# ScalarE's counts of a mask moved apart from its checks of rows, in a four-layer graph kernel

## The chip, the cores and the metric
One core of a Trainium2 chip runs the kernel. The metric is the device time of one execution in microseconds; the times shown are medians of several executions.

## The reference
Four graph layers on x (8 batches, 2048 nodes, 64 channels) share one row-normalised adjacency matrix `adj` (2048 x 2048). Each layer is followed by x = layernorm(x + layer(x)). Cut to what matters:
```
L0: w = einsum(emb, weight); x_g = [x, A x, 2 A (A x) - x]; out = x_g w + b
L1: att = softmax(where(adj > 0.5, leaky_relu(s1 + s2), -9e15)); out = elu(att h)
L2: emb = x W^T + b;  out = ((A + I) emb) / rowsum(A + I)
L3: v = x, row 0 of v set to a given value; 3 times:
        h = relu([v, A v] W1^T + b1);  v = h W2^T + b2
```

## The kernel before, in words
All nonzero values of a row of `adj` are equal in the expected inputs, so the kernel keeps a mask `Bm` in 8-bit floats (0 or 64) with one factor per row, and multiplies by the mask. Since it must be right for other matrices too, it checks this on the way. For each of the 16 blocks of 128 rows (`it` = 0 to 15) ScalarE makes three passes over 2048 columns, each with a sum per row:

- `chk`: counts the mask's entries of block `it` (a Copy of `Bm[:, it, :]` into `junk`, sum in `cnt`);
- then, in the step `sgn`, a Relu of the row block minus the row's maximum (sum in `over`, output into `junk`), and
- a Sign of the same difference (sum in `sg1`, output over the row buffer itself).

The row blocks of `adj` come by a DMA into one buffer, `rowt`. SyncE issues the load of block it + 1 when the Sign of block `it` is done (`s_sign`). `junk` and `rowt` lie in the memory of layer 0's weights and are free when layer 0's last product is done (`s_zp`). After all checks VectorE sums up (`flags`), TensorE adds over partitions (`total`), VectorE decides (`verdict`), and all engines branch: to a slow general program, or to the rest of the fast one.

The order of the work is written out by hand as one list of steps, `MIDDLE` and then `TAIL`. Each engine walks through the whole list in order and issues its own part of every step; semaphores tie the parts together. `last_order` makes `TAIL`. It counts in half-steps of about 4 us: 0 to 31 are layer 2, with the 16 products of the mask, `P` k = 0 to 15 (two half-steps for each, four pieces for each product), and 32 to 115 are layer 3, with the pieces `M` of seven-product sums. `at(y, ...)` puts a step at half-step y, `on(h, ...)` at half-step 32 + h. Steps put at one half-step keep the order in which they were put, the ones left over from `MIDDLE` first.

The steps named below:

- `E` k: takes product k out of PSUM. ScalarE writes the high half into `T`, then VectorE the low half (semaphore `s_zl`). Products have three PSUM banks, and P k waits for E k-3.
- `W` (c, j): TensorE multiplies what E 4c+j made by a weight (it waits for `s_zl`), and VectorE adds it to X.
- `sq`, `red`, `var`, `root`, `rs`, `apply` (L, c, j): the norm of layer L. ScalarE squares, VectorE sums, ScalarE takes the root, VectorE makes the factor and applies it.
- `row_a`, `row_b`, `addrow`: the row that layer 1 adds (an Exp on ScalarE).
- `split` (c, j): when the apply of layer 1 is done, ScalarE writes the high half of X for layer 2's products; GpSimd writes the low half and adds a bias.
- `rows`: nine small steps of VectorE that prepare factors.
- `v0` (c, j): the same halves for layer 3's first input. ScalarE, then GpSimd; TensorE's `D` (c, j) waits for GpSimd's part.
- `G`, `mix`, `cut`, `V`, `t22`: layer 3's passes. G multiplies by a weight and VectorE takes the result out; mix forms the sums; ScalarE and GpSimd cut them into halves; V and t22 take products out of PSUM.

ScalarE's part of chk and sgn before (the whole stands in the listing):
```
elif kind == "chk":
    e.wait_ge(s_zp, 8 * NT)
    if it: e.wait_ge(s_over, it)
    fn(junk, Bm[:, it, :], ACT.Copy, accum_out=cnt[...]).then_inc(s_cnt, 1)
elif kind == "sgn":
    e.wait_ge(s_land, 16 * (it + 1)); ...; e.wait_ge(s_cnt, it + 1)
    fn(junk, rowt, ACT.Relu, ...).then_inc(s_over, 1)
    e.wait_ge(s_over, it + 1)
    fn(rowt, rowt, ACT.Sign, ...).then_inc(s_sign, 1)
```

Of the kernel before, what the change touches and what calls it, by code (L numbers as in the profile page):

```python
# [177 lines left out]
def last_order(after):  # L178
# [42 lines left out]
        at(y + 5, *mixes(n, 1, 4), cut(n, 1, "S1"))  # L221
        at(y + 6, cut(n, 1, "S3"), cut(n, 1, "S4"))
    for it in range(NT):
        at(12 + 4 * it if it < 5 else 32 + 4 * (it - 5) - (it - 5) // 4, ("chk", it))
        at(14 + 4 * it if it < 5 else 34 + 4 * (it - 5) - (it - 5) // 4, ("sgn", it))
    for k in range(16):
        p = pieces("P", k)
        order += late.pop(2 * k, []) + (p[0:2] if k else []) + late.pop(2 * k + 1, []) + (p[2:4] + [("E", k)] if k else [])
    for n in (4, 5, 6, 7):
# [13 lines left out]
        on(h + 14, cut(n, 1, "S1"))  # L243
        on(h + 15, cut(n, 1, "S3"))
        on(h + 16, cut(n, 1, "S4"))
    on(44, ("flags",))
    on(46, ("total",))
    on(47, ("verdict",))

    for n, s, jj, h in ((6, 1, 0, 61), (6, 1, 1, 62), (6, 4, 0, 69), (6, 4, 1, 70), (6, 5, 0, 71), (6, 5, 1, 72), (6, 6, 0, 72),  # L250
                        (6, 6, 1, 73), (7, 1, 0, 75), (7, 1, 1, 76), (7, 4, 0, 80), (7, 4, 1, 81)):
# [50 lines left out]
def gnn_kernel(nc, x_in, at_in, a_in, embt_in, sm_in, bx_in, w0_in, a12_in, w0bb_in, out):  # L302
    ctx = ExitStack()
    with ctx:
# [376 lines left out]
                    RSN[norm_key(x)] = len(RSN)  # L681

        number_norms()

        ORDER3 = [ending(n, s, jj) for n in (6, 7) for s in ENDS for jj in range(2)]

# [379 lines left out]
        def scalar_steps(e, steps):  # L1066
# [3 lines left out]
            for step in steps:  # L1070
# [15 lines left out]
                elif kind == "Z":  # L1086
                    u, t = step[1:]
                    c, j = divmod(u, 4)
                    n4, it = 4 * u + t, 4 * j + t
                    if n4:  # L1090
                        e.wait_ge(s_ab, n4)
                    for g in range(2):
                        e.wait_ge(s_acc[0], 5 * n4 + (3, 5)[g])
                        e.wait_ge(s_acc[1], 5 * n4 + (2, 5)[g])
                        ps = zpair(2 * n4 + g)
                        for d in range(DV, 8):
                            fn(grid(AT[:, 3 * g + d - DV, :]), ps[:, :, d, :], ACT.Copy,
                               scale=emb[:, it, 8 * g + d:8 * g + d + 1]).then_inc(s_za, 1)
                elif kind == "sq":
                    L, c, j = step[1:]  # L1100
                    u = 4 * c + j
                    if L == 0:
                        e.wait_ge(s_add, 4 * u + 4)
                    else:
                        e.wait_ge((None, s_y1, s_y2, s_y3)[L], (order3(c, j) if L == 3 else u) + 1)
                    if L == 3 and summed_by_act(c, j):
                        r = order3(c, j) // 2
                        if r >= 2:
                            e.wait_ge(s_rs, RSN[first_of(*ORDER3[2 * r - 4])] + 1)
                            e.wait_ge(s_sq, SQN[L, c, j])  # L1110
                        o, q = four(sq_buf(L, c, j)), st_part(L, c, j, 0)
                        for i in range(8):
                            t, d = i // 2, slice(64 * (i % 2), 64 * (i % 2) + 64)
                            m = fn(o[:, t, d], X[:, 4 * j + t, 128 * c + d.start:128 * c + d.stop], ACT.Square, accum_out=q[:, i:i + 1])
                        m.then_inc(s_sq, 1)
                        continue
                    if L == 3:
                        e.wait_ge(s_sq, SQN[L, c, j])
                        if order3(c, j) == 15:
                            e.wait_ge(s_red, REDN[(3, *ORDER3[13])] + 1)  # L1120
                    elif SQPREV[L, c, j] is not None:
                        e.wait_ge(s_red, REDN[SQPREV[L, c, j]] + 1)
                    fn(four(sq_buf(L, c, j)), xpart(c, j), ACT.Square).then_inc(s_sq, 1)
                elif kind in ("root", "root3") or kind == "var" and step[1] < 2:
                    L, c, j = (*norm_key(step), 0)[:3]
                    m = 2 if L == 3 else 1
                    e.wait_ge(s_var, VARN[norm_key(step)] + 1)
                    fn(st_part(L, c, j, 1, m), st_part(L, c, j, 2, m), ACT.Sqrt).then_inc(s_sd, 1)
                elif kind == "row_a":
                    e.wait_ge(s_neg, step[1] + 1)  # L1130
                    fn(ROW[:, 1, :], ROW[:, 1, :], ACT.Exp).then_inc(s_exp, 1)
                elif kind == "split":
                    c, j = step[1:]
                    e.wait_ge(s_p2, 4 * c + 4)
                    e.wait_ge(s_n[1], 4 * c + j + 1)
                    fn(spart(0, c, j), xpart(c, j), ACT.Copy).then_inc(s_sh, 1)
                elif kind == "E":
                    k = step[1]
                    c, j = divmod(k, 4)
                    e.wait_ge(s_p, k + 1)  # L1140
                    fn(T[:, c, 0, block(j)], bank(product_bank(k)), ACT.Copy, scale=1.0 / EDGE).then_inc(s_zh, 1)
                elif kind == "V" and step[2] in (0, 2, 6):
                    n, s, jj = step[1:]
                    p = n // 2
                    e.wait_ge(s_p, slot_done(n, s, jj))
                    if RTW[step] is not None:
                        e.wait_ge(s_gl, RTW[step])
                    if n == 2 and s < 6:

                        e.wait_ge(s_red, REDN[2, 1 + s, 3] + 1)  # L1150
                    o, i = RT[rt_buf(s, jj)], bank(pair_bank(n, s, jj))
                    if s == 6:
                        fn(o, i, ACT.Relu, scale=col(cKG + p)).then_inc(s_gt, 1)
                    else:
                        fn(o, i, ACT.Copy, scale=col(cKG + p)).then_inc(s_cp, 1)
                elif kind == "t22":
                    n, jj = step[1:]
                    e.wait_ge(s_t2, 2 * (n - 2) + jj + 1)
                    if RTW[step] is not None:
                        e.wait_ge(s_gl, RTW[step])  # L1160
                    fn(RT[rt_buf(3, jj)], bank(aux_bank[step]), ACT.Copy, scale=col(cKG + n // 2)).then_inc(s_cp, 1)
                elif kind == "cut":
                    n, jj, what = step[1:]
                    if what[0] == "X":
                        e.wait_ge(s_ut, GN[(n // 2, *block_of(n, jj, what))] + 1)
                    else:
                        e.wait_ge(s_mx, MN["mix", n, jj, what] + 1)

                    if what in ("S1", "S2", "S3"):
                        if n > 2:  # L1170
                            e.wait_ge(s_p, slot_done(n - 1, {"S2": 2, "S1": 3, "S3": 4}[what], 1))
                    elif n >= 4:
                        e.wait_ge(s_p, slot_done(n - 2, [x[0] for x in SLOTS].index(what), 1))
                    else:
                        c, j = block_of(n, jj, "X21" if what == "S4" else what)
                        e.wait_ge(s_d, 4 * c + j + 1)
                    fn(half_of(n, what, 0, jj), four(made(n, jj, what)), ACT.Copy).then_inc(s_uh, 1)
                elif kind == "v0":
                    c, j = step[1:]
                    e.wait_ge(s_p, 4 * c + 4)  # L1180
                    e.wait_ge(s_n[2], 4 * c + j + 1)
                    if j == 0:
                        e.wait_ge(s_vt, c + 1)
                        fn(stile(0, 0, c), V0T, ACT.Copy)
                        fn(S[:, 0, 1:4, chunk(c)], X[:, 1:4, chunk(c)], ACT.Copy).then_inc(s_vh, 1)
                    else:
                        fn(spart(0, c, j), xpart(c, j), ACT.Copy).then_inc(s_vh, 1)
                elif kind == "D":
                    c, j = step[1:]
                    e.wait_ge(s_d, 4 * c + j + 1)  # L1190
                    fn(T[:, c, 0, block(j)], bank(aux_bank[step]), ACT.Copy, scale=1.0 / EDGE).then_inc(s_dh, 1)
                elif kind == "chk":
                    it = step[1]
                    e.wait_ge(s_zp, 8 * NT)
                    if it:
                        e.wait_ge(s_over, it)
                    fn(junk, Bm[:, it, :], ACT.Copy, accum_out=cnt[:, it:it + 1]).then_inc(s_cnt, 1)
                elif kind == "sgn":

                    it = step[1]  # L1200
                    e.wait_ge(s_land, 16 * (it + 1))
                    e.wait_ge(s_nr, 1)
                    e.wait_ge(s_cnt, it + 1)
                    fn(junk, rowt, ACT.Relu, bias=nr[:, it:it + 1], accum_out=over[:, it:it + 1]).then_inc(s_over, 1)
                    e.wait_ge(s_over, it + 1)
                    fn(rowt, rowt, ACT.Sign, bias=nr[:, it:it + 1], accum_out=sg1[:, it:it + 1]).then_inc(s_sign, 1)

# [1054 lines left out]
```

## Time and profile before
| what | value |
|---|---|
| median of 3 executions | 1042.79 us (1041.26 to 1042.98) |
| the profiled execution | 1043.06 us, span of its instructions 1041.3 us |
| TensorE busy | 1012.3 us (97%) |
| VectorE busy | 678.1 us (65%) |
| GpSimd busy | 552.9 us (53%) |
| ScalarE busy | 456.8 us (44%) |
| mean granted clock of TensorE | 0.994 |

The busy time of an engine counts its instructions, not its waits. "Idle before", in brackets behind a row of a timeline, is the time in which the engine had nothing to do ahead of that instruction, with the instruction whose end released it. PE is TensorE, ACT is ScalarE, DVE is VectorE, POOL is GpSimd. L1068, L1219 and L1737 are lines of helpers that issue most instructions of ScalarE, VectorE and GpSimd, so a step is recognised by its tiles, its shape and its place in the order.

### The profile page before, as it was taken

The numbers are of one execution on the slowest core, as the hardware profiler recorded it, in microseconds if no ns is written. First come the engines' busy times: TensorE is split into PE (matmuls) and PEld (weight loads), VectorE is DVE, ScalarE is ACT, GpSimd is POOL, SyncE is SP. The second block draws the span as 40 slices with busy tenths as digits, with TensorE's granted clock in tenths as the row PEclk, the third lists the DMA queues.
The fourth block names the chain that finished last, engine by engine and source line by source line (L and its number), as shares of the span: only waits on it lengthen the run. The fifth ranks groups of instructions, "written<-read, shape, count | busy, mean of one in ns | idle before, by whom it ended". The sixth has DMA issues, their size and how long they took to land. (4 is left out here: it accounts for less than half of the span.)

```text
span 1041.3 us, 18648 instructions
## 1 busy us (share of the span) xinstructions
PE 1012.3 (97%) x6854; PEld 486.3 (47%) x6854; DVE 678.1 (65%) x1683; ACT 456.8 (44%) x1109; POOL 552.9 (53%) x645
## 2 busy tenths in 40 slices
PE   7999999999999999999999999999999999999995
PEld 3445444444444444434445556454554545455553
DVE  4877565657566786687667775776584545547556
ACT  4632323333334543444333575584766532232632
POOL 0005497766658798879878374464443242323311
PEclk9999999999999999999999999999999999999998
DMA  9930000000000000000010121121221100000022
GB/s 371 404 127 1 2 1 2 1 2 1 1 1 2 2 1 2 1 2 1 1 42 1 41 82 42 41 82 41 82 82 50 72 1 2 3 2 21 21 62 61
DMA packets 14658, 45.65 MB, mean 44 GB/s; under 512 B 960, under 2 KB 9280, under 8 KB 10080
## 3 DMA queue, kind: packets, MB, share of 16 engines
q1 hardware_dynamic: 14560, 44.39, 11.5%
q8 instruction: 56, 0.92, 0.4%
q14 instruction: 42, 0.34, 0.1%
HBM read 40.19 MB, written 4.19 MB: 43 GB/s over the span
## 5 line engine op out<-in xcount | busy, mean ns | idle before, releaser
L788 PE MATMUL PS<-BW,S 128*128 128x512 fp8e4 x1280 | 291.9, 380 | 0.7 <-DVE R L1219 0.7
L1068 ACT ACTIVATE T<-PS,SM 128x128 f32<-128x128 f32 x384 | 112.8, 365 | 234.3 <-DVE X L1219 155.9
L918 PE MATMUL PS<-WZ,R 64*128 64x512 f16 x1536 | 198.0, 377 | 1.2 <-ACT T L1068 1.2
L788 PEld LDWEIGHTS PS<-BW,S 128*128 128x128 f16 x1280 | 120.6, 98 | 150.3 <-issue 18.2
L955 PE MATMUL PS<-BW,S 128*128 128x512 fp8e4 x768 | 173.1, 379 | 0.6 <-POOL T L1737 0.6
L1737 POOL TENSOR_TENSOR T<-T 128x128 f32<-128x128 f32 (+1 forms) x192 | 124.3, 647 | 74.4 <-ACT T L1068 64.3
L1219 DVE SCALAR_TENSOR_TENSOR X<-PS,SM,X 128x128 f32<-128x128 f32 x320 | 109.5, 342 | 76.4 <-PE PS L918 76.4
L918 PEld LDWEIGHTS PS<-WZ,R 64*128 64x128 f16 x1536 | 69.5, 94 | 104.1 <-issue 26.3
L955 PEld LDWEIGHTS PS<-BW,S 128*128 128x128 f16 x768 | 73.7, 98 | 83.9 <-issue 1.1
L955 PE MATMUL PS<-BW,T 128*128 128x512 fp8e4 x480 | 109.5, 379 | 1.3 <-POOL T L1737 1.3
L1737 POOL TENSOR_TENSOR S<-R,S 128x512 f16<-128x512 f32 (+1 forms) x46 | 52.3, 1144 | 105.6 <-ACT S L1068 105.5
L1219 DVE SCALAR_TENSOR_TENSOR T<-PS,SM,T 128x128 f32<-128x128 f32 x256 | 87.7, 343 | 27.1 <-PE PS L918 27.1
L918 PE MATMUL PS<-WZ,T 64*128 64x512 f16 x768 | 103.8, 376 | 0.0
L1737 POOL TENSOR_TENSOR T<-R,T 128x512 f16<-128x512 f32 x40 | 49.3, 1240 | 87.6 <-DVE T L1211 44.8
L1219 DVE SCALAR_TENSOR_TENSOR R<-PS,cs,R 128x512 f32<-128x512 f32 x48 | 36.0, 749 | 64.1 <-PE PS L955 32.7
L1761 POOL TENSOR_TENSOR BW<-BW 128x512 fp8e4<-128x512 fp8e4 x64 | 70.9, 1113 | 2.7
L955 PEld LDWEIGHTS PS<-BW,T 128*128 128x128 f16 x480 | 46.2, 98 | 54.4 <-POOL T L1737 1.8
L1219 DVE SCALAR_TENSOR_TENSOR R<-PS,ra,R 128x128 f32<-128x128 f32 x176 | 48.8, 342 | 33.6 <-PE PS L775 21.8
L1068 ACT ACTIVATE R<-PS,cs 128x512 f32<-128x512 f32 x48 | 32.6, 679 | 83.7 <-PE PS L782 52.5
L1068 ACT ACTIVATE WZ<-WZ,ra 128x2048 f16<-128x2048 f32 (+1 forms) x32 | 63.9, 1996 | 1.3 <-DMA WZ<-a_in 0.8
L1737 POOL TENSOR_TENSOR X<-X,T 128x128 f32<-128x128 f32 x128 | 58.4, 457 | 10.0
L773 PE MATMUL PS<-hat,T 128*128 128x128 f16 x320 | 57.8, 221 | 4.2 <-DVE T L1219 2.5
(210 smaller groups left out, 1518.9 us busy)
## 6 DMA issues: line engine op xcount, KB each, us to landing
WZ<-a_in SPq DMA_DIRECT2D x16, 1024.0 KB, 4.8
BW<-at_in SPq DMA_DIRECT2D x8, 1024.0 KB, 18.4
R<-at_in SPq DMA_DIRECT2D x7, 1024.0 KB, 12.7
out<-X SPq DMA_DIRECT2D x16, 256.0 KB, 2.3
X<-x_in SPq DMA_DIRECT2D x3, 1024.0 KB, 19.6
T<-w_in SPq DMA_DIRECT2D x1, 1536.0 KB, 15.4
R<-at_in SPq DMA_DIRECT2D x2, 512.0 KB, 4.7
SM<-sm_in SPq DMA_DIRECT2D x1, 520.5 KB, 17.9
```

The lines of the kernel that those rows point to most:

```text
L773: e.matmul(ok, th, hat[:, 0, kind, :], start=True, stop=False)
L788: m = e.matmul(o, stile(h, t, c), Bm[:, t, block(j)], start=(t == 0 and h == 0), stop=(last and t == NT - 1 and h == 1))
L918: m = e.matmul(bank(b0 + q), halves[kd][zh][r, :], WZ[r, wh, kd, block(g)], start=(i == 0), stop=(i == 8))
L955: m = e.matmul(o, half_of(n, what, h, q % 2)[:, t, :], b[:, 4 * (q % 2) + t, :], start=(s in (0, 1, 3) and q % 2 == 0 and t == 0 and h == ...
L1068: return e.activation(o, i, f, **kw)
L1219: return e.scalar_tensor_tensor(out=o, in0=a, scalar=s, in1=b, op0=f, op1=g)
L1737: return e.tensor_tensor(o, a, b, f)
L1761: e.tensor_tensor(o, a, b, f, saturate=False).then_inc(s_bt, 1)
```

## The change: counts early, checks of rows in two steps
The step sgn becomes two, `ovr` (the Relu) and `sgn` (the Sign), and chk, ovr and sgn get other places in the list. In half-steps: chk of block it was at 12, 16, 20, 24, 28, 32, 36, ... and is now at 2 + it, so 2 to 17. ovr and sgn together were two half-steps behind chk (14, 18, ... up to 72); now ovr is at 10, 13, 16, 19 for blocks 0 to 3 and at 51, 53, 56, 58, 61, 64, 66, 69, 71, 74, 77, 79 for the others, and sgn one half-step behind each. `flags`, `total` and `verdict` move from 44, 46 and 47 of layer 3 to 49, 51 and 52; the branch stays at 56. Since chk and ovr both write junk, a function now finds for each of them the one ahead of it in the list, whose semaphore it waits for.
```diff
     for it in range(NT):
-        at(12 + 4 * it if it < 5 else 32 + 4 * (it - 5) - (it - 5) // 4, ("chk", it))
-        at(14 + 4 * it if it < 5 else 34 + 4 * (it - 5) - (it - 5) // 4, ("sgn", it))
+        at(2 + it, ("chk", it))
+        y = 10 + 3 * it if it < 4 else 51 + (13 * (it - 4)) // 5
+        at(y, ("ovr", it))
+        at(y + 1, ("sgn", it))
...
-    on(44, ("flags",))
-    on(46, ("total",))
-    on(47, ("verdict",))
+    on(49, ("flags",))
+    on(51, ("total",))
+    on(52, ("verdict",))
...
+        JUNK = {}
+        def number_junk():
+            held = None
+            for x in TAIL:
+                if x[0] in ("chk", "ovr"):
+                    JUNK[x] = held
+                    held = (s_cnt if x[0] == "chk" else s_over, x[1] + 1)
+        number_junk()
...
                 elif kind == "chk":
                     it = step[1]
                     e.wait_ge(s_zp, 8 * NT)
-                    if it:
-                        e.wait_ge(s_over, it)
+                    if JUNK[step] is not None:
+                        e.wait_ge(*JUNK[step])
                     fn(junk, Bm[:, it, :], ACT.Copy, accum_out=cnt[:, it:it + 1]).then_inc(s_cnt, 1)
-                elif kind == "sgn":
+                elif kind == "ovr":
                     it = step[1]
                     e.wait_ge(s_land, 16 * (it + 1))
                     e.wait_ge(s_nr, 1)
-                    e.wait_ge(s_cnt, it + 1)
+                    e.wait_ge(*JUNK[step])
                     fn(junk, rowt, ACT.Relu, bias=nr[:, it:it + 1], accum_out=over[:, it:it + 1]).then_inc(s_over, 1)
+                elif kind == "sgn":
+                    it = step[1]
                     e.wait_ge(s_over, it + 1)
                     fn(rowt, rowt, ACT.Sign, bias=nr[:, it:it + 1], accum_out=sg1[:, it:it + 1]).then_inc(s_sign, 1)
```

## Rows read from the trace of the kernel before
**Rows 1.** Page, part 1: busy us, share of the span, instructions
```profile
PE 1012.3 (97%) x6854; PEld 486.3 (47%) x6854; DVE 678.1 (65%) x1683; ACT 456.8 (44%) x1109; POOL 552.9 (53%) x645
```
**Rows 2.** TensorE's timeline: start, us, what, [idle before <-released by]
```profile
600.76 0.22 PE L763 MATMUL PS<-dg,S 128*128 128x128 f16 x1 [3.14 <-POOL S L1737]
...
668.49 0.23 PE L773 MATMUL PS<-hat,T 128*128 128x128 f16 x1 [1.69 <-DVE R L1219]
...
686.74 0.39 PE L780 MATMUL PS<-T,hat 128*128 128x512 f16 x1 [0.52 <-DVE T L1219]
...
706.09 0.23 PE L763 MATMUL PS<-dg,S 128*128 128x128 f16 x1 [1.39 <-DVE SM L1219]
...
747.26 1.04 PE L955 MATMUL PS<-BW,T 128*128 128x512 fp8e4 x4 [1.27 <-POOL T L1737]
```
**Rows 3.** Windows: length; PE, PEld, DVE, ACT, POOL busy; granted clock; DMA
```profile
538.64:597.35 58.71, 58.71 (x394) 31.60 (x393) 43.97 (x91) 25.85 (x41) 38.01 (x34) 1.00 0.06 19
...
601.40:604.80 3.40, 3.40 (x18) 1.81 (x16) 1.17 (x2) 2.20 (x4) 1.48 (x2) 0.50 0.24 67
668.50:671.90 3.40, 3.40 (x25) 1.94 (x26) 3.38 (x4) 0.08 (x1) 1.55 (x2) 1.00 0.00 0
```
**Rows 4.** ScalarE's groups by shape, 525 to 860 us: busy, mean ns, idle before
```profile
L1068 ACT ACTIVATE WZ<-BW 128x2048 f16<-128x2048 fp8e4 x16 | 30.4, 1899 | 0.0
...
L1068 ACT ACT_TABLE_LOAD x3 | 3.8, 1283 | 0.1
```
**Rows 5.** ScalarE's timeline, 538 to 597 us (T<-PS is an E, S<-X a split)
```profile
538.64 0.58 ACT L1068 ACTIVATE T<-PS 128x512 f16<-128x512 f32 x1
543.19 0.63 ACT L1068 ACTIVATE S<-X 128x512 f16<-128x512 f32 x1 [3.97 <-DVE X L1531]
...
547.49 0.60 ACT L1068 ACTIVATE T<-PS 128x512 f16<-128x512 f32 x1 [1.14 <-PE PS L938]
...
555.51 0.60 ACT L1068 ACTIVATE T<-PS 128x512 f16<-128x512 f32 x1 [4.86 <-PE PS L938]
559.90 0.63 ACT L1068 ACTIVATE S<-X 128x512 f16<-128x512 f32 x1 [3.79 <-DVE X L1531]
...
564.45 0.60 ACT L1068 ACTIVATE T<-PS 128x512 f16<-128x512 f32 x1 [1.78 <-PE PS L938]
...
569.39 1.90 ACT L1068 ACTIVATE WZ<-BW 128x2048 f16<-128x2048 fp8e4 x1
...
571.28 0.61 ACT L1068 ACTIVATE R<-X 128x512 f32<-128x512 f32 x1
...
573.49 0.58 ACT L1068 ACTIVATE T<-PS 128x512 f16<-128x512 f32 x1
...
577.40 1.99 ACT L1068 ACTIVATE WZ<-WZ,ra 128x2048 f16<-128x2048 f32 x1
...
581.51 0.57 ACT L1068 ACTIVATE T<-PS 128x512 f16<-128x512 f32 x1
...
590.86 0.31 ACT L1068 ACTIVATE S<-R 128x128 f16<-128x128 f32 x1 [2.91 <-DVE R L1219]
...
596.30 1.67 ACT L1068 ACTIVATE S<-X 128x512 f16<-128x512 f32 x3 [4.23 <-DVE X L1531]
```
**Rows 6.** VectorE's timeline: E 4, and the squares' sum after the long idle time
```profile
558.52 0.69 DVE L1219 SCALAR_TENSOR_TENSOR T<-PS,T 128x512 f16<-128x512 f32 x1
...
659.60 0.69 DVE L1222 TENSOR_REDUCE T<-R 128x8 f32<-128x512 f32 x1 [5.24 <-ACT R L1068]
```
**Rows 7.** GpSimd's timeline: low half of split(3,1), then v0(0,1) and v0(0,2)
```profile
597.00 1.16 POOL L1737 TENSOR_TENSOR S<-X,S 128x512 f16<-128x512 f32 x1 [2.55 <-ACT S L1068]
...
599.46 2.27 POOL L1737 TENSOR_TENSOR S<-X,S 128x512 f16<-128x512 f32 x2
```
**Rows 8.** DMA issues: KB each, median us from issue to landing
```profile
WZ<-a_in SPq DMA_DIRECT2D x16, 1024.0 KB, 4.8
```

## The prediction, made before the changed kernel ran
> **What bounds the kernel now.** I read the page's busy times first: TensorE is busy for 97% of the span and ScalarE for 44% [rows 1]. So TensorE's work sets the time, the change takes none of it away, and only what TensorE waits for can change. I next looked through TensorE's timeline for idle time behind the point where layer 2 begins (about 525 us). The reader is to see five waits there [rows 2]: 3.14 us at 600.76, and 1.69, 0.52, 1.39 and 1.27 us at 668.49, 686.74, 706.09 and 747.26. The first one costs more than its length: from 601.40 to 604.80 the granted clock is 0.50, the 1.2 GHz level, and 3.4 us of work at half speed are 1.7 us of loss; after the wait of 1.69 us it stays at 1.00, the 2.4 GHz level [rows 3]. Then I read ScalarE's own timeline where layer 2 begins [rows 5], because it is the only engine whose order changes, and beside it the steps of VectorE and GpSimd that hand work back and forth with it [rows 6, 7].
>
> **What the change moves.** No operation is added or dropped. ScalarE still runs 16 counts (chk) and 16 pairs (ovr, sgn). A count takes 1.90 us [rows 4] and holds the queue for 1.9 us (569.39 to 571.28); a pair holds it for 4.1 us (577.40 to 581.51), so about 2.1 and 2.0 us for its halves [rows 5]. What changes is which steps stand behind them. All 16 counts go to half-steps 2 to 17, two before nearly every E k, the step that takes product k out of PSUM. Pairs 0 to 3 go to half-steps 10 to 20, none follows up to 50, and the other 12 go to 51 to 80.
>
> **What goes away.** Between half-steps 21 and 50 ScalarE has no checks, and the four later waits lie there. Take the one at 668.49: VectorE had stood idle for 5.24 us until 659.60, for a square that ScalarE had behind pair 4; it caught up too late for the PSUM bank that TensorE wanted [rows 2, 6]. Without that pair (4.1 us) VectorE comes some 2.8 us earlier there, more than the 1.69 us. The waits at 706.09 and 747.26 follow pairs 6 and 8 in the same way, and the short one pair 5. I take all four away: 1.69 + 0.52 + 1.39 + 1.27 = 4.87 us.
>
> **What the 16 counts cost.** ScalarE has 58.71 - 25.85 = 32.9 us of idle time between E 1 and the row v0(0,1) [rows 3], and looks able to hide them. But VectorE takes its steps in order too. In a loop that runs through the window, ScalarE's E k lets VectorE do its E k and then an apply, which lets ScalarE do its next split; behind that split the new order puts two counts, and E k+1 behind them. A count ahead of an E therefore delays the loop itself, and the wait for VectorE's apply comes afterwards just as before. I carried the delay along the queue, starting from the times in [rows 5]:
> - E 1 (538.64) has two counts ahead: +3.8 us. VectorE's E 1, its rs and apply move by as much, so split(2,0) goes from 543.19 to 547.0.
> - E 2 has two more: +7.6. E 3 has two more, but had been waiting for TensorE, so 547.49 becomes 557.6: +10.1.
> - E 4 (555.51) has two more, less its old idle time: +8.9. VectorE comes to it only behind the step rows, which moved by 10.1, so it goes on at 568.6 in place of 558.52 [rows 6], and split(2,3) at 570.0 in place of 559.90.
> - E 5 (564.45) has ovr 0, count 8, sgn 0 and count 9 ahead, 7.9 us: it comes at 580.6, +16.1.
> - E 6 (573.49) has count 10, ovr 1 and count 11 ahead: 590.8, +17.4.
> - E 7 (581.51) has sgn 1 and counts 12 and 13 ahead, and lost the old pair 0: 600.5, +19.0.
> - v0(0,0) (590.86) has ovr 2 and count 14 ahead, in place of one count: +19.0. E 8 has sgn 2 and count 15: 614.4.
> - VectorE then makes the row for split(3,1), which goes from 596.30 to 616.4: +20.1.
>
> GpSimd follows as in [rows 7]: low half and bias of split(3,1) from 597.00, low half of v0(0,1) from 599.46 (half of 2.27 us, so to 600.6), which is what released TensorE at 600.76. All of it moves by 20.1 us. TensorE can run ahead only in part: W(1,0) needs E 4 and stands right behind product 5 (whose end is E 5's old start, 564.45), W(1,1) needs E 5 behind product 6, and so on. So the time will not be lost in one place. I expect waits of about 4.3 us before W(1,0), 4.6 before W(1,1), 2.3 before W(1,2), 1.7 before W(1,3), and about 10.6 in D(0,0) and D(0,1); the last includes the old 3.14. The sum over the old waits is 20.1 us.
> Two adjacent operations on the junk buffer also wait for each other. Where ovr and Sign do so now, 2.1 us lie between them and only 2.0 behind, so I add 0.1 us at each of 8 such places: 0.8 us.
>
> **What could come behind it.** After 21 us of delay TensorE is behind ScalarE's remaining work by more than before (E 9 moves by about 18 us), and only pair 3 is left there, so I book no new wait up to half-step 50. The clock: several waits are now over 3.14 us, but what is lost after the earlier ones is waited out anyway; the last costs 1.7 us as it does today. Zero net, and at most another 1.7 us if it stays low twice as long. In half-steps 51 to 80 pairs come every 2.6 half-steps, and five times ovr stands one half-step behind the Sign that frees the row buffer. A row needs 4.8 us to land [rows 8], so ScalarE waits 3 to 4 us there and cuts come up to 9 us later. The PSUM evictions among them move by 3 us or less, and the cuts are wanted 15 us or more later; the kernel of before has no wait of TensorE there at all between 750 and 900 us though each pair holds 4.1 us in one piece. I take nothing, and 4 us as the upper end. flags, total and verdict move five half-steps, some 20 us; the verdict is at 52 and the branch at 56, so four half-steps of cover (some 16 us) are left: nothing.
>
> On the activation tables, first the trace: a load takes 1.28 us, with three in this stretch [rows 4], and after the last one all Sign and Sqrt steps run on it. Sign 0 now stands between the row step's Exp and the Sqrt of var(1,3), so that last load may only come earlier, ahead of sgn 0, where the queue is full; that would be 1.3 us more. The Trainium skill, page "ScalarE: Activation LUTs", section "What ACT_TABLE_LOAD costs", puts a switch of sets at 2.66 us with its drain, by which it would be 2.7 us. The trace has 1.28. I leave it out of the sum and in the range.
>
> **Sum.** 20.1 + 0.8 - 4.9 = +16.0 us. The profiled execution took 1043.06 us around its span of 1041.3, so it becomes 1059.1; it was 0.27 us above the median of 1042.79, so I predict 1059.
>
> **Rivals.**
> *Hidden counts, so the kernel gets faster.* If VectorE and GpSimd absorb the delays, that is if the 32.9 us of idle time really take the counts, only ScalarE's full queue counts: 25.85 - 7.9 (checks that are there now) + 16 x 1.95 + 3 x 4.2 = 61.8 us against 58.71, and v0(0,1) comes 3.1 us later. Then 3.1 - 4.9 = -1.8: 1041. It decides below a delay of 4.9 us. For it speaks ScalarE's idle time; against it that each idle stretch in [rows 5] sits behind a step which waits for VectorE, and that VectorE's step waits for the E behind the counts. If the old wait of 3.14 went too, with its clock loss, 1033. Chance 0.10.
> *No measurable change.* A delay of 3 to 7 us, eaten by the 4.9: 1041 to 1045. Chance 0.05.
> *Half absorbed.* Work that TensorE's waits give room for shortens VectorE's steps, and the delay is 8 to 13 us: 1046 to 1051. Chance 0.13.
> *Forecast.* In-order queues pass it all on: 1052 to 1063. Chance 0.64.
> *The late pairs cost too.* The waits for rows in half-steps 51 to 80 reach TensorE, or the table load does: 16.0 + 4 + 1.3 = 21: 1064. Chance 0.08.
>
> **The numbers.** A difference under 0.2% (2 us) can't be told from none here. Faster 0.11, same 0.04, slower 0.85. The range goes from 1046, below which are the first two rivals, to 1064.
>
> **What would show it.** In the profile after: TensorE's waits before the W products between 565 and 600, and a long one until GpSimd's low half of v0(0,1) near 620; ScalarE nearly without idle time from 565 to 615; no waits where the four were. If the first wait is still near 601 and about 3 us long, the loop argument is wrong, and the kernel is level or faster.

## The result, and the profile after

The changed kernel takes 1054.06 us (median of 4 executions, 1053.1 to 1055.02), beside 1042.52 us for the kernel before on the same chip: a ratio of 1.0114, with an interval of 1.0099 to 1.013. It is slower by 11.5 us, where +16.0 was forecast. The profiled execution took 1055.02 us, around a span of 1053.2.

The page's busy times of the kernel after, as in [rows 1]:
```profile
PE 1014.5 (96%) x6854; PEld 487.7 (46%) x6854; DVE 673.6 (64%) x1683; ACT 457.0 (43%) x1109; POOL 553.4 (53%) x645
```
The instruction counts are the same as before. The span is 11.9 us more than 1041.3. TensorE is idle for 1053.2 - 1014.5 = 38.7 us, before for 29.0: +9.7. Its busy time rose by 2.2, and 9.7 + 2.2 = 11.9.

TensorE's timeline of the kernel after, all its waits behind the start of layer 2; they answer to [rows 2]:
```profile
565.85 0.22 PE L788 MATMUL PS<-hat,T 128*128 128x128 f16 x1 [1.13 <-issue]
...
578.48 0.22 PE L788 MATMUL PS<-hat,T 128*128 128x128 f16 x1 [4.44 <-issue]
...
588.70 0.22 PE L788 MATMUL PS<-hat,T 128*128 128x128 f16 x1 [0.36 <-issue]
...
598.59 0.22 PE L788 MATMUL PS<-hat,T 128*128 128x128 f16 x1 [1.70 <-issue]
...
608.78 0.22 PE L778 MATMUL PS<-dg,S 128*128 128x128 f16 x1 [2.02 <-POOL S L1755]
...
617.50 0.26 PE L778 MATMUL PS<-dg,S 128*128 128x128 f16 x1 [8.11 <-POOL S L1755]
```
The first four rows are the W products (their input is T), the last two D(0,0) and D(0,1). Together they wait 17.76 us where 3.14 stood, +14.6. Behind 617.50 there is none up to 900: the four waits of 4.87 us in all are gone. 14.6 - 4.9 = +9.7, the idle time above. The word "issue" must not be taken to mean that nothing was waited for. VectorE's timeline in the same stretch:
```profile
565.06 0.69 DVE L1237 SCALAR_TENSOR_TENSOR T<-PS,T 128x512 f16<-128x512 f32 x1
...
577.68 0.69 DVE L1237 SCALAR_TENSOR_TENSOR T<-PS,T 128x512 f16<-128x512 f32 x1 [3.79 <-ACT T L1083]
```
These are VectorE's parts of E 4 and E 5. They end at 565.75 and 578.37, and the W products start 0.10 and 0.11 us later: the W steps waited for `s_zl`. The second row also names what VectorE had waited for: ScalarE's part of E 5.

ScalarE's timeline, kernel after; it answers to [rows 5]:
```profile
538.28 1.90 ACT L1083 ACTIVATE WZ<-BW 128x2048 f16<-128x2048 fp8e4 x1
...
540.36 1.91 ACT L1083 ACTIVATE WZ<-BW 128x2048 f16<-128x2048 fp8e4 x1
...
542.26 0.58 ACT L1083 ACTIVATE T<-PS 128x512 f16<-128x512 f32 x1
545.54 0.63 ACT L1083 ACTIVATE S<-X 128x512 f16<-128x512 f32 x1 [2.70 <-DVE X L1549]
...
566.44 0.63 ACT L1083 ACTIVATE S<-X 128x512 f16<-128x512 f32 x1 [2.25 <-DVE X L1549]
567.09 1.28 ACT L1083 ACT_TABLE_LOAD   x1
568.38 0.31 ACT L1083 ACTIVATE ROW<-ROW 128x128 f32<-128x128 f32 x1
...
573.20 1.99 ACT L1083 ACTIVATE WZ<-WZ,ra 128x2048 f32<-128x2048 f32 x1
...
577.08 0.57 ACT L1083 ACTIVATE T<-PS 128x512 f16<-128x512 f32 x1
...
587.89 1.28 ACT L1083 ACT_TABLE_LOAD   x1
...
613.03 1.67 ACT L1083 ACTIVATE S<-X 128x512 f16<-128x512 f32 x3 [1.42 <-DVE X L1549]
```
Two counts (BW into WZ, which here is Bm into junk) stand ahead of E 1 at 542.26, and ahead of split(2,0) at 545.54 ScalarE still waits 2.70 us for VectorE's apply: the counts did not fill that gap, they moved it. (It was 3.97 us before; the 1.27 us between are VectorE's step rs, which took that much less.) The last row is split(3,1), 16.7 us later than in [rows 5]. GpSimd's low halves behind it, which release D(0,1), answer to [rows 7]:
```profile
613.74 1.15 POOL L1755 TENSOR_TENSOR S<-X,S 128x512 f16<-128x512 f32 x1 [3.60 <-ACT S L1083]
...
616.19 3.39 POOL L1755 TENSOR_TENSOR S<-X,S 128x512 f16<-128x512 f32 x3
```

Windows around the last two waits and the second one, kernel after (stretch, length, busy us of PE, PEld, DVE, ACT, POOL with instruction counts, granted clock, DMA share, GB/s); they answer to [rows 3]:
```profile
538.28:613.57 75.29, 61.46 (x396) 32.35 (x394) 40.37 (x91) 59.97 (x76) 36.96 (x33) 0.95 0.12 43
...
609.70:617.50 7.80, 0.00 (x0) 0.03 (x1) 3.99 (x8) 6.38 (x9) 4.12 (x5) 0.50 0.37 134
617.50:623.30 5.80, 5.80 (x29) 3.41 (x30) 3.82 (x6) 3.79 (x8) 4.37 (x4) 0.50 0.00 0
578.90:582.40 3.50, 3.50 (x16) 1.58 (x14) 3.16 (x10) 2.72 (x4) 2.61 (x3) 0.51 0.14 59
```
The clock is at 0.50, the 1.2 GHz level, for 3.4 us behind the wait of 4.44, and from 609.7 to 623.4, the last 5.9 us of it with work. ScalarE is busy for 59.97 of 75.29 us from its first count to split(3,1): over the whole stretch it was not full. From 565 to 615, where the prediction wanted it nearly without idle time, it is busy for 41.38 of 50 us.

The stretch behind D(0,1), first the kernel before, then the kernel after, with the same 2714 matmuls:
```profile
600.76:1041.30 440.54, 423.91 (x2714) 222.82 (x2714) 272.76 (x614) 217.31 (x490) 169.74 (x143) 0.98 0.13 44
...
617.50:1053.20 435.70, 424.45 (x2714) 223.93 (x2714) 271.66 (x614) 182.80 (x455) 170.96 (x143) 0.98 0.12 40
```
D(0,1) starts 16.7 us later, and from there to the end the kernel is 4.8 us shorter: 16.7 - 4.8 = 11.9, the growth of the span.

### The profile page after: what moved, and what is told of

It is laid out like the page before. It is cut to its first block, busy times and chain, and to the rows that moved or that the text cites. A ratio compares the mean times of both kernels' runs of the same rounds, so it can differ in the third digit from the quotient of the medians.

```text
span 1053.2 us, 18648 instructions
## 1 busy us (share of the span) xinstructions
PE 1014.5 (96%) x6854; PEld 487.7 (46%) x6854; DVE 673.6 (64%) x1683; ACT 457.0 (43%) x1109; POOL 553.4 (53%) x645
## 4 chain that ended last, share of the span: by engine, by line
PE 80%; DVE 9%; ACT 6%; issue 2%; DMA 2%; POOL 1%; SPq 0%; ACTq 0%; DVEq 0%; POOLq 0%
PE PS L970 27%; PE PS L933 23%; PE PS L803 20%; ACT WZ L1083 3%; DMA BW<-at_in 2%; PE PS L788 2%; PE PS L790 2%; PE PS L789 2%; DVE BW L1234 1%; DVE T L1237 1%; DVE X L1549 1%; PE PS L797 1%; PE PS L795 1%; PE PS L796 1%; DVE X L1237 1%
## 5 line engine op out<-in xcount | busy, mean ns | idle before, releaser
L1083 ACT ACTIVATE WZ<-WZ,ra 128x2048 f16<-128x2048 f32 (+1 forms) x32 | 63.8, 1993 | 27.5 <-DMA WZ<-a_in 27.5
L788 PE MATMUL PS<-hat,T 128*128 128x128 f16 x320 | 58.2, 221 | 10.1 <-issue 7.6
L1237 DVE SCALAR_TENSOR_TENSOR T<-PS,T 128x512 f16<-128x512 f32 x48 | 32.0, 686 | 53.0 <-ACT T L1083 48.0
## 6 DMA issues: line engine op xcount, KB each, us to landing
SM<-sm_in SPq DMA_DIRECT2D x1, 520.5 KB, 17.8
```

The lines of the kernel that those rows point to most:

```text
L788: e.matmul(ok, th, hat[:, 0, kind, :], start=True, stop=False)
L1083: return e.activation(o, i, f, **kw)
L1237: return e.scalar_tensor_tensor(out=o, in0=a, scalar=s, in1=b, op0=f, op1=g)
```

## The experiments

Each kernel was compared with the kernel before on the same chip. The kernel before read 1042.1 to 1042.5 us in all of these comparisons, so differences of a few tenths between two rows of the table mean nothing. "Shift" is how much later split(3,1) starts than the 596.30 of [rows 5], in us; the last column is TensorE's last wait before 625, in us.

| kernel | median us | ratio, interval | shift | last wait |
|---|---|---|---|---|
| after | 1054.06 | 1.0114, 1.0099 to 1.013 | +16.7 | 8.11 |
| e1 counts behind E | 1046.8 | 1.0042, 1.0025 to 1.0059 | +9.9 | 8.27 |
| e2 no counts | 1036.72 | 0.9937, 0.9919 to 0.9954 | +0.26 | 3.02 |
| e3 pairs only | 1036.41 | 0.994, 0.9924 to 0.9957 | +0.25 | 3.02 |
| e4 counts only | 1053.81 | 1.0108, 1.0091 to 1.0125 | +12.6 | 7.06 |
| e5 one behind E | 1039.7 | 0.9976, 0.9967 to 0.9986 | +2.2 | 5.32 |
| e6 one ahead of E | 1044.61 | 1.0026, 1.0016 to 1.0037 | +8.0 | 8.11 |
| e7 mask sums later | 1039.46 | 0.9972, 0.9963 to 0.9982 | -1.6 | 1.15 |
| e8 pairs, D later | 1032.73 | 0.9909, 0.9896 to 0.9923 | -0.17 | 1.34 |
| e9 e8 and e7 | 1033.18 | 0.9917, 0.9903 to 0.9931 | -1.75 | 1.4 |

**e1, the two counts directly behind E k.** On the kernel after:
```diff
-        at(2 + it, ("chk", it))
...
+        if 1 <= k <= 8:
+            order += [("chk", 2 * k - 2), ("chk", 2 * k - 1)]
```


> The changed kernel, but each pair of counts stands directly behind its E k (k = 1 to 8) in place of ahead of it; the same 16 counts beside the same products, pairs as changed. Loop theory (what costs is that a count stands between ScalarE's split and the E that VectorE waits for): VectorE gets its E at once and makes the apply while ScalarE counts, so split(3,1) comes about 8 us earlier than in the changed kernel, the waits of TensorE before W products shrink to under 3 us in all, and the time is 1043 to 1048 us. Rival, ScalarE's load (its queue is simply full in that stretch, wherever the counts stand): as the changed kernel, 1052 to 1055 us.

The split comes 6.8 us less late than in the kernel after, and the kernel is 7.3 us faster, with the same load on ScalarE beside the same products. So load alone doesn't explain the loss. But order alone doesn't either: the split is still 9.9 us late. ScalarE's timeline of e1 at split(2,0) and split(2,1) shows no wait for VectorE any more where 3.97 and 1.42 us stood, since two counts fill more than that:
```profile
542.79 0.63 ACT L1084 ACTIVATE S<-X 128x512 f16<-128x512 f32 x1
...
547.79 0.61 ACT L1084 ACTIVATE S<-X 128x512 f16<-128x512 f32 x1
```
The waits at the W products shrink to 1.1 us in all. The long wait at D(0,1) stays, in TensorE's timeline of e1:
```profile
610.64 0.26 PE L779 MATMUL PS<-dg,S 128*128 128x128 f16 x1 [8.27 <-POOL S L1756]
```

**e2, no counts at all.** This kernel leaves out the 16 counts; `flags` then takes a difference of `sg1` with itself, so the check of the mask's entries isn't made.
```diff
-        at(2 + it, ("chk", it))
...
-                    e.wait_ge(s_cnt, NT)
-                    fc(stt(e, cw2, cnt, 1.0 / EDGE, sg1, ALU.mult, ALU.subtract))
+                    fc(stt(e, cw2, sg1, 1.0, sg1, ALU.mult, ALU.subtract))
```


> The changed kernel without the 16 counts of the mask (that part of the check is left out, and the sum over it is made from zero). Loop theory: pairs 0 to 3 at half-steps 10 to 20 cost TensorE nothing new (the old wait of about 3 us near 600 stays), and the four later waits stay away: 1036 to 1039 us, so the counts' price is 15 to 18 us. Rival, the pairs at half-steps 10 to 20 are a good part of the loss: 1042 us or more.

TensorE's only wait from 560 to 900 is the old one:
```profile
601.03 0.22 PE L777 MATMUL PS<-dg,S 128*128 128x128 f16 x1 [3.02 <-POOL S L1754]
```
Against the kernel after, the 16 counts cost 1054.06 - 1036.72 = 17.3 us, and what is left of the change, the moved pairs, gains 5.5.

**e3, the pairs only.** The counts back at their old places, pairs and flags as changed.
```diff
-        at(2 + it, ("chk", it))
+        at(12 + 4 * it if it < 5 else 32 + 4 * (it - 5) - (it - 5) // 4, ("chk", it))
...
```


> Only ovr and sgn (and flags, total, verdict) go to their new places; the counts stay at 12, 16, 20, ... as before. Loop theory: ahead of split(3,1) stand 12.4 us of halves of pairs and 3.8 us of counts in place of 7.9 us, partly taken by idle time: 4 to 6 us later; the four later waits (4.9 us) go: 1040 to 1044 us, no difference from before that can be told. Rival, half-steps 51 to 80 are too full with counts and halves of pairs waiting for rows to land: new waits of TensorE there, 1045 us or more.

I missed the size: 1036.41, faster than expected. I had put the split 4 to 6 us later. The halves of pairs 0 to 2 put E 5 and E 6 2.6 and 2.4 us later, but E 7 only 0.3 and v0(0,0) 0.25: idle time took it all up. The wait at D(0,1) is the old one, 3.02 us at 601.01 as in e2, and the later ones are gone. It takes as long as e2, which has no counts. So with the pairs moved, the 16 counts cost nothing at their old places and 17.3 us at their new ones.

**e4, the counts only.** Counts as changed; ovr, sgn, flags, total and verdict at their old places.
```diff
-        y = 10 + 3 * it if it < 4 else 51 + (13 * (it - 4)) // 5
-        at(y, ("ovr", it))
-        at(y + 1, ("sgn", it))
+        at(14 + 4 * it if it < 5 else 34 + 4 * (it - 5) - (it - 5) // 4, ("ovr", it), ("sgn", it))
...
```


> Only the counts go to half-steps 2 to 17; each pair, flags, total and verdict stay where they were. Loop theory: up to v0(0,1) the queue lacks ovr and sgn 1 and 2 (8 us) of the changed kernel, so TensorE passes D(0,1) 8 to 10 us later than before, not 16.7, and of the later waits most stay, as they come from pairs: 1048 to 1053 us. Rival, the later waits come from the sum of checks and go with the counts: 1046 us or less.

The shift was 12.6, more than the 8 to 10 that I had put down, and the time 0.8 us over the upper end. TensorE's timeline of e4 has the long wait, and the first of the four later ones again:
```profile
613.39 0.26 PE L776 MATMUL PS<-dg,S 128*128 128x128 f16 x1 [7.06 <-POOL S L1753]
...
681.36 0.23 PE L786 MATMUL PS<-hat,T 128*128 128x128 f16 x1 [1.70 <-DVE R L1235]
```
So the removal of those waits is the pairs' doing. From here to the kernel after, three pairs stand ahead of split(3,1) in place of one, some 8 us of work, of which 4.1 us arrive in the shift; and e4's later waits go (1.70, 0.51, 1.03 and 0.28, 3.5 us in all); the two times agree within 0.3 us.

**e5 and e6, one count behind or ahead of E k.** Both have the pairs as changed, one count at each of E 1 to E 15 and the 16th at the start of layer 3. They differ by the order of two neighbours on ScalarE alone.
In e5, behind the line that appends E k:
```diff
-        at(2 + it, ("chk", it))
...
+        if k:
+            order.append(("chk", k - 1))
...
+    on(0, ("chk", 15))
```
In e6 the list of the two steps `[("chk", k - 1), ("E", k)]` stands in the place of E k instead.


> The changed kernel with one count per product, directly behind E k (k = 1 to 15, the 16th at the start of layer 3), pairs as changed. Loop theory: 1.9 us of count fit into ScalarE's idle time behind nearly every E (3.97, 1.42, 1.42, 3.79 us before the splits), so split(3,1) comes 0 to 4 us later than before: 1036 to 1041 us. Rival, ScalarE's load from ovr and sgn 0 to 3 plus any counts there is what costs: half the counts beside the pairs, half the loss, 1045 us.

> The same as the run with one count per product behind E k, but each count directly ahead of E k. The load on ScalarE is the same, only the order of two neighbours differs. Loop theory: each count ahead of an E delays VectorE's E by 1.9 us wherever ScalarE has no idle time before it, so split(3,1) comes 6 to 10 us later than before, 4 us or more later than with the counts behind: 1041 to 1047 us. Rival, load: no difference between the two.

Both came out as expected. e6 loses 4.9 us to e5, from one swap. And e5, against e1, says what the number of counts is worth when all stand behind E: one for each product in place of two is 7.1 us faster (1039.7 against 1046.8). ScalarE's timeline, first e5:
```profile
538.66 0.58 ACT L1085 ACTIVATE T<-PS 128x512 f16<-128x512 f32 x1
539.14 1.90 ACT L1085 ACTIVATE WZ<-BW 128x2048 f16<-128x2048 fp8e4 x1
...
543.22 0.63 ACT L1085 ACTIVATE S<-X 128x512 f16<-128x512 f32 x1 [2.08 <-DVE X L1551]
543.75 0.58 ACT L1085 ACTIVATE T<-PS 128x512 f16<-128x512 f32 x1
```
and e6:
```profile
538.72 1.89 ACT L1083 ACTIVATE WZ<-BW 128x2048 f16<-128x2048 fp8e4 x1
...
540.61 0.58 ACT L1083 ACTIVATE T<-PS 128x512 f16<-128x512 f32 x1
543.88 0.63 ACT L1083 ACTIVATE S<-X 128x512 f16<-128x512 f32 x1 [2.70 <-DVE X L1549]
544.41 1.89 ACT L1083 ACTIVATE WZ<-BW 128x2048 f16<-128x2048 fp8e4 x1
...
546.31 0.57 ACT L1083 ACTIVATE T<-PS 128x512 f16<-128x512 f32 x1
```
Behind E 1 the count runs while VectorE works towards the apply, and E 2 starts at 543.75. Ahead of E 1 it runs while VectorE waits for E 1, the wait of 2.70 us for the apply comes on top, and E 2 starts at 546.31.

**e7, the sums of the mask later.** This one asks why the delay was smaller than forecast. It is the kernel before, with 16 of GpSimd's mask sums (`bt`) moved out of the stretch.
```diff
-        at(i - 46, ("bt", i))
+        at(i - 46 + 16, ("bt", i))
```


> The kernel before, with GpSimd's last 16 mask sums (bt 48 to 63, 1.1 us each) put 16 half-steps later; everything else as before. Theory: VectorE's small steps (rs, rows) are slow while GpSimd works beside them, so in this run the step rows takes 3.5 to 4.5 us in place of 6.2 and rs(1,2) 1.2 to 1.6 us in place of 2.5. Rival, they take as long for another reason (their own waits on each other): unchanged. The time: within 2 us of before, since E 4 and E 5 wait for TensorE anyway.

It is 2.7 us faster, where I had given it at most 2, and the step rows came out shorter than the 3.5 to 4.5 us that I expected. GpSimd has nothing to do from 553.09 to 558.68, while VectorE makes most of the step rows, and VectorE's timeline of e7 reads
```profile
554.07 0.31 DVE L1212 TENSOR_SCALAR R<-SM,cs 128x64 f32<-128x64 f32 x1
554.42 0.67 DVE L1212 TENSOR_SCALAR R<-c1row,cs 128x64 f32<-128x64 f32 x2
```
The same three instructions in the kernel before, VectorE's timeline:
```profile
555.11 1.27 DVE L1212 TENSOR_SCALAR R<-SM,cs 128x64 f32<-128x64 f32 x1
556.42 2.07 DVE L1212 TENSOR_SCALAR R<-c1row,cs 128x64 f32<-128x64 f32 x2
```
and GpSimd's beside them:
```profile
555.07 1.26 POOL L1737 TENSOR_TENSOR X<-X,bc 128x512 f32<-128x512 f32 x1
556.29 2.15 POOL L1761 TENSOR_TENSOR BW<-BW 128x512 fp8e4<-128x512 fp8e4 x2
```
VectorE's 0.31 us become 1.27, and it ends at 556.38, 0.05 us behind GpSimd's instruction, which began just ahead of it. The whole step rows takes 6.17 us before, 3.63 after and 2.39 in e7; rs(1,2) takes 2.51, 1.24 and 1.24. TensorE's wait at D(0,1) is 1.15 us here in place of 3.14, and the clock stays at 1.00 behind it. The Trainium skill, page "SBUF — State Buffer", section "Who interferes with whom", says that VectorE and GpSimd share a pair of ports under an exclusive lock, so that whichever comes second waits for the other's whole instruction, and that `tensor_scalar` can be such an instruction. The rows of this case agree: they have VectorE's short instruction ending with GpSimd's long one.

**e8 and e9, on from e3.** Since e3's only wait was D(0,1) for GpSimd, e8 puts the first four D steps one half-step (about 4 us) later, so that TensorE does other pieces first. e9 adds the edit of e7.
```diff
-        at(y + 5, ("D", c, 0), ("D", c, 1))
-        at(y + 6, ("D", c, 2), ("D", c, 3))
+        z = c == 0
+        at(y + 5 + z, ("D", c, 0), ("D", c, 1))
+        at(y + 6 + z, ("D", c, 2), ("D", c, 3))
```


> The run in which only the pairs moved, with TensorE's D(0,0) to D(0,3) one half-step later, so that GpSimd's low half of v0(0,1) is there first. Theory: the wait of 3.0 us at 601 and the 3.4 us at half clock behind it are the last thing to be had in this stretch: 1031 to 1033 us, the clock stays at 1.00 up to the end. Rival, the wait moves to the next step that needs these halves (G, then the cuts of layer 3): 1036 us as with the pairs alone.

> The fastest run so far (pairs moved, counts where they were, D(0,*) one half-step later) with GpSimd's last 16 mask sums 16 half-steps later as well. What the two give overlaps: both work on the wait near 600, which is gone already. If only the 1.34 us before W at 624 are left to be had: 1031 to 1033 us. Rival, GpSimd's sums now fall beside the cuts of layer 3's first sums, and make new waits there: 1034 us or more.

Both came as expected. e8 takes 1032.73 us, 0.9% less than the kernel before, and with e9, which can't be told from it, is the fastest of all. Its window across the stretch, with the granted clock at 1.00 throughout:
```profile
560.00:640.00 80.00, 78.66 (x591) 44.87 (x589) 59.47 (x132) 53.97 (x82) 49.75 (x44) 1.00 0.15 54
```
The second edit gains nothing more: a wait of 1.34 us at 624.12 (e8) and of 1.4 us at 624.62 (e9) is all that either has from 560 to 900.

## Why the prediction was right, point by point

- **Direction and place held, and the loop is shown, but it is not the whole cause.** The waits stood where they were forecast, at the W products and in D(0,0) and D(0,1). Without the counts the price of 17.3 us is gone (e2), with them at their old places too (e3). The order of neighbours alone is worth 4.9 us (e5 against e6) or 7.3 (e1 against the kernel after). But the order explains only part. From the kernel after to e3 it is 17.65 us in three steps: 7.3 for the order (to e1), 7.1 for one count at each product in place of two (e1 to e5), and 3.3 for the way from there to the old places (e5 to e3), which no run takes apart. How many counts fall on each turn of the loop so matters as much as on which side of E they stand. The prediction charged both together, count by count, and had no separate price for either.
- **The step that was mis-sized** is the delay of split(3,1), "from 596.30 to 616.4: +20.1", with its 0.8 for adjacent junk operations. It measured +16.7, so the delay less the later waits is 16.7 - 4.8 = 11.9 where the forecast had 20.1 + 0.8 - 4.9 = 16.0. The rest of the sum held. Along the hand-made chain E 1 was +3.6 (3.8 forecast), E 2 +6.3 (7.6), E 3 +9.1 (10.1), E 4 +8.1 (8.9), E 5 +12.6 (16.1), E 6 +13.8 (17.4), E 7 +15.7 (19.0). Nearly all of the error arises up to E 5. I had moved VectorE's steps with the durations of the kernel before. But rs(1,2) took 1.24 in place of 2.51 us and rows 3.63 in place of 6.17, 3.8 us less, because less of GpSimd's work fell beside them. e7 shows the same shortening in the kernel before, with GpSimd's work taken away. So "VectorE goes on at 568.6" became 565.06. VectorE's timeline of the kernel after at that place:
```profile
563.11 0.86 DVE L1229 TENSOR_SCALAR R<-SM,cs 128x128 f32<-128x128 f32 x1
564.01 0.31 DVE L1230 TENSOR_SCALAR R<-SM,cs 128x64 f32<-128x64 f32 x1
564.36 0.66 DVE L1230 TENSOR_SCALAR R<-c1row,cs 128x64 f32<-128x64 f32 x2
```
and GpSimd's:
```profile
561.75 2.15 POOL L1779 TENSOR_TENSOR BW<-BW 128x512 fp8e4<-128x512 fp8e4 x2
```
The instruction at 563.11 ends at 563.97, just behind GpSimd's at 563.90; the next three run at their short durations. The wait at W(1,0) was therefore 1.13 us, not 4.3. The waits came to 17.8 us in all, where the forecast's five items add up to 23.5; over the old 3.14 that is 14.6 against its "20.1" (its own items give 20.4). The rival "half absorbed" had named this mechanism, shorter steps of VectorE, but expected a delay of 8 to 13 us.
- **The four later waits** went entirely, -4.87, as forecast, and e4, which keeps the old pairs, keeps them.
- **The clock** was booked at zero net with 1.7 on top as a bound. Zero net is what came. TensorE's busy time rose by 2.2 us, but 1.6 of it lie ahead of D(0,1) (590.00 against 588.38 us), where the 3.4 us at 0.50 behind the wait of 4.44 are: D(0,1) starts when GpSimd releases it, so slower work there only shortens the wait, as forecast. Behind D(0,1) 5.9 us of work run at 0.50, where 3.4 did in [rows 3], which by these figures is an estimated 1.25 us more of loss. But busy time there rose by only 0.5 us, and the stretch as a whole is 4.8 us shorter, as much as the four waits that are gone. What makes up for the difference isn't shown.
- **The late pairs** cost nothing, as forecast, though ScalarE did wait for its rows. Its groups by line, kernel after:
```profile
L1083 ACT ACTIVATE WZ<-WZ,ra 128x2048 f16<-128x2048 f32 x16 | 31.9, 1996 | 27.5 <-DMA WZ<-a_in 27.5
```
The 16 ovr steps waited 27.5 us in all for the landing, 4.3 at most, and TensorE had no wait there. flags, total and verdict cost nothing either.
- **The table load** didn't come earlier: Sign 0 ran at 573.20 on the set loaded at 567.09 for the Exp, and the next load still stands at 587.89, behind E 6. The possible 1.3 us fell away. The split ahead of the load at 567.09 ends at 567.07, and the Exp follows 1.29 us behind the load's start. The Trainium skill, page "ScalarE: Activation LUTs", section "What ACT_TABLE_LOAD costs", has 2.66 us for a switch, 1.28 of load and 1.38 of drain. The load agrees; no drain is seen on either side of it, and the measurement decides.
- **The pairs' halves in layer 2** stood in the chain at full price ahead of E 5 to E 7, and ovr 2 at nothing ahead of v0(0,0). On their own they are absorbed (e3: +0.25). On the queue filled by the counts some 8 us of halves add 4.1 us (after against e4): E 5 comes 3.8 us later than in e4, while ScalarE's idle time ahead of v0(0,0) shrinks from 2.91 to 0.73 us. The forecast was for that case and right in kind, but the halves are no fixed cost.
- **Two slips** of the prediction changed nothing: the sum of the waits above, and the 1033 us for "if the old wait went too", which from its own 1041 would be 1036.

## What to carry to other kernels

Idle time of an in-order engine is not free for filler work: ask what stands behind the new instruction, and whether the engine's next wait is for something that this very instruction delays. Put filler directly behind the step that releases the other engine, never ahead of it, and no more of it per turn of the loop than the idle stretch there holds: here one count of 1.9 us behind each E cost 3.3 us over e3, two cost 10.4. When delays are carried along by hand, short VectorE instructions should be priced as they run alone and as they run beside GpSimd, since a shift changes which of the two holds. And a wait at the head of TensorE's queue may be cheaper to avoid by placing the waiting step one half-step later (3.7 us from e3 to e8) than by speeding up what it waits for.

## What the runs showed of the hardware

- VectorE's `tensor_scalar` on 128x64 fp32 takes 0.31 us alone and 1.0 to 1.27 us beside GpSimd, ending together with GpSimd's instruction. GpSimd's load so sets the length of VectorE's small steps: rows took 2.39, 3.63 or 6.17 us.
- The granted clock fell to 0.50 for 3.4 us behind a wait of 3.14 us, for 13.7 us around the waits of 2.02 and 8.11 us, for as long in e1 (waits of 3.19 and 8.27), for 6.8 us in e5 (5.32), and not at all behind waits of 1.69 and 2.52 us (the latter in e7).
- Sign ran without a load on the set that Exp had loaded as well as on the one for Sqrt.
